# Mask, scale and row maximum of attention scores as one VectorE instruction per tile

## The chip, the cores and the metric

The kernel runs on one core of a Trainium2 chip. The metric is the device time of one execution in microseconds (us); the median of three runs is shown for the kernel before.

## The reference, cut to what matters

The input x has 4 sequences of 512 tokens with 512 features. Each token is normalised (layer norm), and the result goes two ways.

- Causal attention with 16 heads of 128 features: `scores = q @ k.T / sqrt(128)`, masked scores are set to -1e5, `attn = softmax(scores)`, `z = attn @ v`, and the heads are summed through `W_O`.
- A gated feed-forward network of 1408 hidden features with ternary weights, `silu(g) * u`, projected back and passed through silu.

The output is `x + attention * silu(ffn)`. All inputs and the output are f32.

## The kernel before, in words

The feed-forward part comes first (about the first 270 us). Then come 64 attention **units**, one for each pair of sequence and head. Every f32 operand of a matmul is held as two f16 parts, "hi" and "lo", and a product is three f16 matmuls. ScalarE (ACT) writes the hi part, VectorE (DVE) writes the lo part as the difference.

TensorE (PE) runs in `unit(u)`: the projections Q and K of head u+1 (`project_head`), V of a later tile (`project_v(u + 4)`), the scores of head u+1 (`scores`), an output projection (`project_out_tile(u - 4)`) and last `weigh_v(u)`, the product of the softmax of head u with V. So the softmax of a head has about one unit of time before PE needs it. Before `scores`, PE waits for the exponentials of the head before (`exp_ok`) and for Q and K of this head (`q_lo`, `k_lo`). `weigh_v` waits for two DMA transposes of the probabilities, hi (`pt_ok[0]`) and lo (`pt_ok[1]`).

The causal scores of one head lie in three PSUM banks as four tiles, listed in `SCORE_TILES` in the order in which PE writes them: query block 3 (512 wide, first bank), query block 2 (384 wide, second bank), query block 0 (128 wide, the rest of the second bank), query block 1 (256 wide, third bank). `score_mm` counts three steps for them, because block 2 gives no signal of its own.

The softmax of a head passes through these steps, and the queues of the engines hold them in this order:

- DVE `maxima`: add the mask on the diagonal blocks (L1056, three instructions), reduce each tile to its row maximum (L1062, four), multiply the maxima by the negative scale (L1066, two: tile 0 alone, then the other three together).
- ACT `exps`: four exponentials from PSUM with `neg_max` as bias and a row sum (L824). Then ACT `split_probs`: the hi part of the probabilities (L837, four).
- DVE `invert_sums` (L1072, two), then `add_out` (L1094, the output accumulation, which also releases GpSimd), then DVE `split_probs`: the lo part (L1080, four).
- SyncE (SP) issues the two transposes (L335) when all hi parts and then all lo parts are there. It also loads one slice of weights for each unit.
- Behind them on DVE come the lo parts of Q (L1040) and K (L1043) of the next head, of Z (L1087), of V (L1049) and of a weight slice (L898).

Units 60 to 62 have no V projection, and in them the lo part of Z (L1087) comes ahead of the lo parts of Q and K. Unit 60's output projection waits for it.

GpSimd (POOL) fetches x and the parked feed-forward result for finished tiles from about 900 us on, combines them with two elementwise instructions for each tile (L383, L386) and stores them. For the last four tiles it prepares a base with eight instructions in a row (L414, L416). At the start it builds `ident` and `mask`.

Of the kernel before, what the change touches and what calls it, by code (L numbers as in the profile page):

```python
# [28 lines left out]
ALU = mybir.AluOpType  # L29
ACT = mybir.ActivationFunctionType  # L30
AX_X = mybir.AxisListType.X
F32 = mybir.dt.float32
# [3 lines left out]
P = 128  # L36
B, S, D = 4, 512, 512
# [4 lines left out]
TT = S // P  # L42
# [7 lines left out]
WS = 16.0  # L50
SCORE_SCALE = float(E) ** -0.5 / WS ** 2
MASKED = -1.0e5 / SCORE_SCALE
EPS = 1e-5


SCORE_TILES = [(3, 0, 0, 0), (2, 1, 0, 512), (0, 1, 384, 896), (1, 2, 0, 1024)]
P_AT = {i: at for i, _, _, at in SCORE_TILES}

DIAGONALS = [(0, 384, 1), (1, 256, 2), (2, 128, 1)]

# [20 lines left out]
def build(nc, x, ffn_w, attn_w, cols, b_o, down_s, out):  # L83
# [7 lines left out]
    with ExitStack() as ctx:  # L91
        def sb(name, shape, dt):
            return ctx.enter_context(nc.sbuf_tensor(name, shape, dt))

        def sem(name):
            return ctx.enter_context(nc.semaphore(name))
# [10 lines left out]
        fw, at = carve(group, 2 * MT * 3 * 512)  # L107
        FW = [fw.rearrange("p (s m w n) -> p s m w n", s=2, m=MT, w=3)[:, part] for part in (0, 1)]
        x_in, at = carve(at, TT * D, F32)
        ffn_in, at = carve(at, 2 * 3 * 512, F32)  # L110
        silu_gate, at = carve(at, S, F32)
        hidden, at = carve(at, S, F32)
        ht, at = carve(at, 2 * 3 * S)
# [40 lines left out]
        K = [sb(f"K_{n}", [P, S], F16) for n in ("hi", "lo")]  # L154
        w_in = sb("w_in", [P, 2, 512], F32)
        ident = sb("ident", [P, P], F32)
        mask = sb("mask", [P, 2, P], F32)
        cols_in = sb("cols_in", [P, 3 * H + 2 * MT], F32)
        biases = sb("biases", [P, 3 * H], F32)
        ffn_scales = sb("ffn_scales", [P, 2 * MT], F32)  # L160
# [12 lines left out]
        newton_a = sb("newton_a", [P, TT], F32)  # L173
        newton_b = sb("newton_b", [P, TT], F32)
        rstd = sb("rstd", [P, TT], F32)
        row_max = sb("row_max", [P, TT], F32)
        neg_max = sb("neg_max", [P, TT], F32)
        row_sum = sb("row_sum", [P, TT], F32)
        inv_sum = sb("inv_sum", [P, TT], F32)
# [62 lines left out]
        out_mm = sem("out_mm")  # L242
        out_added = sem("out_added")
        score_mm = sem("score_mm")
        masked = sem("masked")
        maxed = sem("maxed")
        negated = sem("negated")
        exp_ok = sem("exp_ok")
        inverted = sem("inverted")
        p_hi = sem("p_hi")  # L250
# [100 lines left out]
        @block.gpsimd  # L351
        def _(pool):
            nc.gpsimd.memset(ident[:], 0.0).then_inc(blank_ok, 1)
            nc.gpsimd.memset(mask[:], 0.0).then_inc(blank_ok, 1)
            nc.gpsimd.memset(ones[:], 1.0).then_inc(ident_ok, 1)
            pool.wait_ge(blank_ok, 2)
            nc.gpsimd.affine_select(out=ident[:], in_=ident[:], compare_op=ALU.not_equal, fill=1.0, base=0,
                                    pattern=[[-1, P]], channel_multiplier=1).then_inc(ident_ok, 1)
            nc.gpsimd.affine_select(out=mask[:], in_=mask[:], compare_op=ALU.is_ge, fill=MASKED, base=0,
                                    pattern=[[0, 2], [-1, P]], channel_multiplier=1).then_inc(ident_ok, 1)  # L360
            pool.wait_ge(const_loaded, 48)
            nc.gpsimd.tensor_scalar(ffn_scales[:], cols_in[:, 3 * H:], 1.0 / WS, None, ALU.mult).then_inc(const_scaled, 1)
            nc.gpsimd.tensor_scalar(biases[:], cols_in[:, 0:3 * H], WS, None, ALU.mult).then_inc(const_scaled, 1)
            nc.gpsimd.tensor_scalar(down_rows[:], down_rows[:], 1.0 / WS, None, ALU.mult).then_inc(const_scaled, 1)

            pool.wait_ge(score_mm, 1)
            for part in (0, 1):
                for at, blocks in GAPS:
                    nc.gpsimd.memset(P_SPLIT[part][:, at:at + blocks, :], 0.0).then_inc(gaps_ok, 1)
            pool.wait_ge(park_done, 16 * B)  # L370
            with pool.Fori(0, T // P) as t:
                nc.gpsimd.tensor_copy(acc[:, t], b_o_rows[:]).then_inc(acc_ready, 1)


            def load_tail(t, par):
                pool.dma_start(x_again[:, par], x_tiles[t]).then_inc(tail_loaded[par], 16)
                pool.dma_start(silu_again[:, par], parked_tiles[t]).then_inc(tail_loaded[par], 16)

            def finish(t, par, turns):

                pool.wait_ge(tail_loaded[par], 32 * turns)
                pool.wait_ge(out_added, TAIL_ADDED + t + 1)
                nc.gpsimd.tensor_tensor(silu_again[:, par], acc[:, t], silu_again[:, par],  # L383
                                        ALU.mult).then_inc(tail_mul, 1)
                pool.wait_ge(tail_mul, t + 1)
                nc.gpsimd.tensor_tensor(silu_again[:, par], silu_again[:, par], x_again[:, par],  # L386
                                        ALU.add).then_inc(tail_add, 1)
                pool.wait_ge(tail_add, t + 1)
                pool.dma_start(out_tiles[t], silu_again[:, par]).then_inc(stored[par], 16)

            def refill(t, par, turns):
                pool.wait_ge(stored[par], 16 * turns)
                load_tail(t, par)

            pool.wait_ge(v_mm, TAIL_ADDED)
            pool.wait_ge(q_mm, TAIL_ADDED)
            for par in range(2):
                load_tail(par, par)
            with pool.Fori(0, TT // 2) as i:
                for par in range(2):  # L400
                    finish(2 * i + par, par, i + 1)
                    refill(2 * i + par + 2, par, i + 1)


            pool.dma_start(x_last, x_chunks[B - 1]).then_inc(last_loaded, 16)
            pool.dma_start(silu_last, parked_chunks[B - 1]).then_inc(last_loaded, 16)
            with pool.Fori(TT // 2, TT) as i:
                for par in range(2):
                    finish(2 * i + par, par, i + 1)
                    refill(2 * i + par + 2, par, i + 1)  # L410

            pool.wait_ge(last_loaded, 32)
            for t in range(TT):
                nc.gpsimd.tensor_tensor(acc[:, TAIL + t], acc[:, TAIL + t], silu_last[:, t], ALU.mult).then_inc(base_mul, 1)  # L414
                pool.wait_ge(base_mul, t + 1)
                nc.gpsimd.tensor_tensor(acc[:, TAIL + t], acc[:, TAIL + t], x_last[:, t], ALU.add).then_inc(base_ok, 1)  # L416
            for par in range(2):
                finish(2 * TT + par, par, TT + 1)
                refill(2 * TT + par + 2, par, TT + 1)
            for par in range(2):  # L420
                finish(TAIL - 2 + par, par, TAIL // 2)
            for t in (0, 1):
                pool.wait_ge(last_mul, t + 1)
                nc.gpsimd.tensor_tensor(silu_last[:, t], silu_last[:, t], acc[:, TAIL + t],
                                        ALU.add).then_inc(pool_sum, 1)
            for par in range(2):
                pool.wait_ge(stored[par], 16 * (TAIL // 2))
# [274 lines left out]
        def _(act):  # L702
# [114 lines left out]
                nc.scalar.activation(V[0][:, (t // TT) % 2, t % TT, :], v_bank(t)[:], ACT.Copy).then_inc(v_hi, 1)  # L817

            def exps(n):
                for i, b_, col, at in SCORE_TILES:  # L820
                    width = (i + 1) * P
                    if i >= TT - 2:
                        act.wait_ge(negated, 2 * n + TT - i)
                    e = nc.scalar.activation(probs[:, at:at + width], SC[b_][:, col:col + width], ACT.Exp,  # L824
                                             bias=neg_max[:, i:i + 1], scale=SCORE_SCALE,
                                             accum_out=row_sum[:, i:i + 1])
                    if i in (TT - 1, 1):
                        e.then_inc(exp_ok, 1)
# [54 lines left out]
        def _(dve):  # L883
# [167 lines left out]

            def maxima(n):

                for b_, col, blocks in DIAGONALS:
                    dve.wait_ge(score_mm, 3 * n + b_ + 1)
                    nc.vector.tensor_tensor(SC[b_][:, col:col + blocks * P], SC[b_][:, col:col + blocks * P],  # L1056
                                            mask[:, 0:blocks, :].rearrange("p b k -> p (b k)"),
                                            ALU.add).then_inc(masked, 1)
                for g, (i, b_, col, _) in enumerate(SCORE_TILES):
                    if g < 3:  # L1060
                        dve.wait_ge(masked, 3 * n + g + 1)
                    nc.vector.reduce_max(row_max[:, i:i + 1], SC[b_][:, col:col + (i + 1) * P], AX_X).then_inc(maxed, 1)  # L1062
                    if g in (1, TT - 1):
                        dve.wait_ge(maxed, TT * n + (1 if g == 1 else TT))
                        cols_ = slice(TT - 1, TT) if g == 1 else slice(0, TT - 1)
                        nc.vector.tensor_scalar(neg_max[:, cols_], row_max[:, cols_], -SCORE_SCALE, None,  # L1066
                                                ALU.mult).then_inc(negated, 1)

            def invert_sums(n):
                for half, cols_ in enumerate((slice(TT - 1, TT), slice(0, TT - 1))):  # L1070
# [118 lines left out]
```

## Time and profile before

| | |
|---|---|
| time, median of 3 runs | 1154.16 us (1153.47 to 1157.09) |
| span of the profiled execution | 1154.1 us, mean granted TensorE clock 0.995 |
| PE matmul busy | 1125.5 us, 98% |
| DVE busy | 729.6 us, 63% |
| ACT busy | 575.7 us, 50% |
| POOL busy | 84.1 us, 7% |
| chain that ended last | PE 88%, DVE 3%, DMA 3%, ACT 3%, issue 2% |

The profile gives no time of its own for that execution beside the span from its first to its last instruction. Busy time is what an engine spent in instructions. The chain that ended last follows the work back from the last instruction, at each step to what released it, so it names what set the end.

### The profile page before, as it was taken

To read this page: it belongs to the slowest core of one execution; us is meant where nothing else is said; L and a number is where in the kernel's file an instruction comes from. 1 tells how busy PE (TensorE), PEld (TensorE's weight loads), DVE (VectorE), ACT (ScalarE), POOL (GpSimd) and SP (SyncE) were. 2 spreads that over 40 slices of the span, in tenths; PEclk is the share of its full clock that TensorE was granted. 3 is DMA by queue.
4 is the path that set the end of the run, shared out by engine and by line. 5 is a ranking of instruction groups with operands and counts; after the bars stand their busy time and mean duration, and the time that the engine had idled before them with its cause. 6 is when DMAs were issued, how large, how long until landed. Compare 5 with 4: busy or idle time off the path is not lost.

```text
span 1154.1 us, 23252 instructions
## 1 busy us (share of the span) xinstructions
PE 1125.5 (98%) x5772; PEld 547.8 (47%) x5772; DVE 729.6 (63%) x1587; ACT 575.7 (50%) x1276; POOL 84.1 (7%) x104
## 2 busy tenths in 40 slices
PE   5999999999999999999999999999999999999987
PEld 3344444444444544544444545444445454554443
DVE  6665364435776666666666666666666666677775
ACT  5754353334565544555455545555555444455532
POOL 1000000003000000000000000000000000134373
PEclk9999999999999999999999999999999999999989
DMA  6401111112444334333444334333444633346545
GB/s 227 167 30 43 45 56 55 55 48 64 97 92 89 82 77 82 82 77 77 85 89 87 77 77 86 77 77 80 88 90 80 114 60 59 86 114 187 118 118 132
DMA packets 236756, 101.77 MB, mean 88 GB/s; under 512 B 219456, under 2 KB 219456, under 8 KB 236736
## 3 DMA queue, kind: packets, MB, share of 16 engines
q1 hardware_dynamic: 231200, 85.78, 33.9%
q0 software_dynamic: 3424, 11.54, 3.3%
q10 hardware_dynamic: 2112, 4.19, 1.0%
q8 instruction: 12, 0.20, 0.1%
q14 instruction: 8, 0.07, 0.0%
HBM read 38.57 MB, written 8.39 MB: 41 GB/s over the span
## 4 chain that ended last, share of the span: by engine, by line
PE 88%; DVE 3%; DMA 3%; ACT 3%; issue 2%; SPq 0%; ACTq 0%; DVEq 0%
PE bank L436 79%; PE bank L589 8%; DMA arena<-arena 2%; PE bank L449 1%; ACT arena L824 1%; ACT arena L837 1%; DMA arena<-ffn_w_dram 1%; DVE row_max L1062 1%; DVE arena L1080 0%; SPq L335 0%; DMA arena<-x_dram 0%; DVE bank L1056 0%; DVE arena L888 0%; ACT V_hi L817 0%; DVE arena L1147 0%
## 5 line engine op out<-in xcount | busy, mean ns | idle before, releaser
L436 PE MATMUL bank<-XT_hi,arena 128*128 (+1 forms) x1392 | 453.3, 380 | 2.8 <-issue 2.7
L436 PE MATMUL bank<-XT_lo,arena 128*128 (+1 forms) x864 | 328.0, 380 | 0.0
L436 PE MATMUL bank<-arena 128*128 (+1 forms) x1124 | 268.3, 380 | 1.2 <-DVE arena L1087 1.0
L824 ACT ACTIVATE arena<-bank,neg_max 128x512 f32<-128x512 f32 (+3 forms) x256 | 132.6, 524 | 216.2 <-DVE neg_max L1066 216.1
L436 PEld LDWEIGHTS bank<-XT_hi,arena 128*128 (+1 forms) x1392 | 136.4, 98 | 161.9 <-issue 7.0
L436 PEld LDWEIGHTS bank<-arena 128*128 (+1 forms) x1124 | 107.6, 98 | 126.2 <-issue 13.4
L436 PE MATMUL bank<-arena,XT_hi 128*128 (+1 forms) x512 | 152.3, 379 | 0.0
L1080 DVE SCALAR_TENSOR_TENSOR arena<-arena,inv_sum 128x512 f16<-128x512 f32 (+3 forms) x256 | 144.2, 625 | 4.3 <-ACT arena L837 4.3
L436 PEld LDWEIGHTS bank<-XT_lo,arena 128*128 (+1 forms) x864 | 84.7, 98 | 92.7 <-issue 0.8
L837 ACT ACTIVATE arena<-arena,inv_sum 128x512 f16<-128x512 f32 (+3 forms) x256 | 122.3, 558 | 0.8 <-DVE inv_sum L1072 0.8
L589 PE MATMUL bank<-arena,V_hi 128*128 128x512 f16 x504 | 111.0, 301 | 3.3 <-DMA arena<-arena 3.0
L1062 DVE TENSOR_REDUCE row_max<-bank 128x1 f32<-128x512 f32 (+3 forms) x256 | 111.1, 481 | 0.0
L436 PE MATMUL bank<-arena,XT_lo 128*128 (+1 forms) x256 | 97.0, 379 | 0.0
L813 ACT ACTIVATE K_hi<-bank,biases 128x512 f16<-128x512 f32 x64 | 44.0, 687 | 100.6 <-PE bank L436 100.5
L1043 DVE SCALAR_TENSOR_TENSOR K_lo<-bank,biases,K_hi 128x512 f16<-128x512 f32 x64 | 48.0, 750 | 72.2 <-ACT K_hi L813 72.2
L817 ACT ACTIVATE V_hi<-bank 128x512 f32 (+1 forms) x64 | 38.2, 597 | 91.4 <-PE bank L436 91.4
L1049 DVE TENSOR_TENSOR V_lo<-bank,V_hi 128x512 f32 (+1 forms) x64 | 44.3, 692 | 58.8 <-ACT V_hi L817 58.8
L957 DVE SCALAR_TENSOR_TENSOR arena<-bank,ffn_scales,arena 128x512 f32<-128x512 f32 x44 | 33.0, 751 | 74.8 <-PE bank L436 65.5
L436 PEld LDWEIGHTS bank<-arena,XT_hi 128*128 (+1 forms) x512 | 50.0, 98 | 60.4 <-DVE V_lo L1049 0.2
L436 PE MATMUL bank<-K_hi,Q_hi 128*128 128x512 f16 (+3 forms) x256 | 74.0, 302 | 3.7 <-DVE K_lo L1043 3.7
L436 PE MATMUL bank<-K_lo,Q_hi 128*128 128x512 f16 (+3 forms) x256 | 77.3, 302 | 0.0
L1072 DVE RECIPROCAL inv_sum<-row_sum 128x1 f32<-128x1 f32 (+1 forms) x128 | 21.6, 170 | 86.9 <-ACT arena L824 80.0
(83 smaller groups left out, 1085.8 us busy)
## 6 DMA issues: line engine op xcount, KB each, us to landing
w_in<-attn_w_dram SPq DMA_DIRECT2D x64, 256.0 KB, 2.6
arena<-ffn_w_dram SPq DMA_DIRECT2D x11, 768.0 KB, 5.3
arena<-x_dram SPq DMA_DIRECT2D x16, 256.0 KB, 4.0
parked_silu<-arena ACTq DMA_DIRECT2D x4, 1024.0 KB, 4.5
arena<-x_dram POOLq DMA_DIRECT2D x12, 256.0 KB, 2.9
arena<-parked_silu POOLq DMA_DIRECT2D x12, 256.0 KB, 3.0
out_dram<-arena POOLq DMA_DIRECT2D x12, 256.0 KB, 2.8
arena<-arena SPq DMA_TRANSPOSE x128, 4.2
```

Of the source, the lines that this page charges most:

```text
L436: mm = nc.tensor.matmul(out, stationary(a, k), moving(b, k), start=first and n == 0 and i == 0, stop=last and n == len(tiles) - 1 and i == ...
L589: return nc.tensor.matmul(ZB[:, j * P:], V[a][:, (u // HG) % 2, j, ds((u % HG) * E, E)], PT[b][:, (J_STEP + 1) * j:J_STEP * j + TT, :].rea ...
L813: nc.scalar.activation(K[0][:], KB[:], ACT.Identity, bias=bias_of(1, n)).then_inc(k_hi, 1)
L817: nc.scalar.activation(V[0][:, (t // TT) % 2, t % TT, :], v_bank(t)[:], ACT.Copy).then_inc(v_hi, 1)
L824: e = nc.scalar.activation(probs[:, at:at + width], SC[b_][:, col:col + width], ACT.Exp, bias=neg_max[:, i:i + 1], scale=SCORE_SCALE, accu ...
L837: nc.scalar.activation(query_blocks(0, i), probs_by_block(i, at), ACT.Copy, scale=inv_sum[:, i:i + 1]).then_inc(p_hi, 1)
L957: nc.vector.scalar_tensor_tensor(out=hidden, in0=UP[:], scalar=ffn_scales[:, ds(MT + m, 1)], in1=silu_gate, op0=ALU.mult, op1=ALU.mult).th ...
L1043: nc.vector.scalar_tensor_tensor(out=K[1][:], in0=KB[:], scalar=bias_of(1, n), in1=K[0][:], op0=ALU.add, op1=ALU.subtract).then_inc(k_lo, 1)
L1049: nc.vector.tensor_tensor(V[1][:, at, t % TT, :], v_bank(t)[:], V[0][:, at, t % TT, :], ALU.subtract).then_inc(v_lo, 1)
L1062: nc.vector.reduce_max(row_max[:, i:i + 1], SC[b_][:, col:col + (i + 1) * P], AX_X).then_inc(maxed, 1)
L1072: nc.vector.reciprocal(inv_sum[:, cols_], row_sum[:, cols_]).then_inc(inverted, 1)
L1080: nc.vector.scalar_tensor_tensor(out=query_blocks(1, i), in0=probs_by_block(i, at), scalar=inv_sum[:, i:i + 1], in1=query_blocks(0, i), op ...
```

## The change

`maxima` has one instruction for each of the four tiles in place of three mask additions, four reductions and two small multiplications. The new instruction adds the mask to the whole tile, multiplies by the negative scale, writes the result in place in PSUM and keeps the minimum of each row, starting at `NO_MIN`. The exponential then uses a scale of -1. The mask grows from two diagonal blocks to a row of 512 columns whose last 128 are the diagonal block and the rest zero, so a tile of any width takes its last columns. Ahead of three of the four instructions DVE waits for the scores and counts up a semaphore `minimizing` that nobody waits for. The exponential of tile 1 now waits for tile 2 as well, since both lie in one bank.

```diff
+NO_MIN = 3.0e38
-DIAGONALS = [(0, 384, 1), (1, 256, 2), (2, 128, 1)]
+MAX_AFTER = [1, 2, 2, 3]
+EXP_AFTER = [1, 3, 3, 4]
...
-        mask = sb("mask", [P, 2, P], F32)
+        mask = sb("mask", [P, S], F32)
...
-            nc.gpsimd.affine_select(out=mask[:], in_=mask[:], compare_op=ALU.is_ge, fill=MASKED, base=0,
-                                    pattern=[[0, 2], [-1, P]], channel_multiplier=1).then_inc(ident_ok, 1)
+            nc.gpsimd.affine_select(out=mask[:, S - P:], in_=mask[:, S - P:], compare_op=ALU.is_ge, fill=MASKED, base=0,
+                                    pattern=[[-1, P]], channel_multiplier=1).then_inc(ident_ok, 1)
...
             def exps(n):
-                for i, b_, col, at in SCORE_TILES:
+                for g, (i, b_, col, at) in enumerate(SCORE_TILES):
                     width = (i + 1) * P
-                    if i >= TT - 2:
-                        act.wait_ge(negated, 2 * n + TT - i)
+                    if g != 2:
+                        act.wait_ge(maxed, TT * n + EXP_AFTER[g])
                     e = nc.scalar.activation(probs[:, at:at + width], SC[b_][:, col:col + width], ACT.Exp,
-                                             bias=neg_max[:, i:i + 1], scale=SCORE_SCALE,
+                                             bias=neg_max[:, i:i + 1], scale=-1.0,
                                              accum_out=row_sum[:, i:i + 1])
...
             def maxima(n):
 
-                for b_, col, blocks in DIAGONALS:
-                    dve.wait_ge(score_mm, 3 * n + b_ + 1)
-                    nc.vector.tensor_tensor(SC[b_][:, col:col + blocks * P], SC[b_][:, col:col + blocks * P],
-                                            mask[:, 0:blocks, :].rearrange("p b k -> p (b k)"),
-                                            ALU.add).then_inc(masked, 1)
                 for g, (i, b_, col, _) in enumerate(SCORE_TILES):
-                    if g < 3:
-                        dve.wait_ge(masked, 3 * n + g + 1)
-                    nc.vector.reduce_max(row_max[:, i:i + 1], SC[b_][:, col:col + (i + 1) * P], AX_X).then_inc(maxed, 1)
-                    if g in (1, TT - 1):
-                        dve.wait_ge(maxed, TT * n + (1 if g == 1 else TT))
-                        cols_ = slice(TT - 1, TT) if g == 1 else slice(0, TT - 1)
-                        nc.vector.tensor_scalar(neg_max[:, cols_], row_max[:, cols_], -SCORE_SCALE, None,
-                                                ALU.mult).then_inc(negated, 1)
+                    width = (i + 1) * P
+                    if g != 2:
+                        dve.wait_ge(score_mm, 3 * n + MAX_AFTER[g])
+
+                        dve.sem_inc(minimizing, 1)
+                    nc.vector.tensor_tensor_reduce(
+                        out=SC[b_][:, col:col + width], in0=SC[b_][:, col:col + width], in1=mask[:, S - width:],
+                        scale=-SCORE_SCALE, scalar=NO_MIN, op0=ALU.add, op1=ALU.min,
+                        accum_out=neg_max[:, i:i + 1]).then_inc(maxed, 1)
```

## Rows read from the trace of the kernel before

**Rows 1.** The page's first part: busy time, share of the span, instructions.
```profile
PE 1125.5 (98%) x5772; PEld 547.8 (47%) x5772; DVE 729.6 (63%) x1587; ACT 575.7 (50%) x1276; POOL 84.1 (7%) x104
```

**Rows 2.** The chain that ended last: start us, us, what.
```profile
340.07 11.99 PE bank L436 x60
...
869.62 1.63 PE bank L589 x12
```

**Rows 3.** Waits of PE over the span: us in total, times, longest us.
```profile
PE bank L449 <- DVE arena L920: 9.8, 1, 9.8
PE bank L436 <- DVE K_lo L1043: 3.7, 3, 3.4
PE bank L589 <- DMA arena<-arena: 3.0, 3, 1.6
```

**Rows 4.** Timeline of DVE in a steady unit: start us, us, instruction.
```profile
704.89 0.82 DVE L1056 TENSOR_TENSOR bank<-bank,mask 128x128 f32<-128x128 f32 x3
...
707.39 0.17 DVE L1066 TENSOR_SCALAR neg_max<-row_max 128x3 f32<-128x3 f32 x1
...
714.00 0.75 DVE L1043 SCALAR_TENSOR_TENSOR K_lo<-bank,biases,K_hi 128x512 f16<-128x512 f32 x1 [1.35 <-ACT K_hi L813]
```

**Rows 5.** Timeline of ACT and of PE in the same unit.
```profile
706.86 0.69 ACT L824 ACTIVATE arena<-bank,neg_max 128x512 f32<-128x512 f32 x1 [3.32 <-DVE neg_max L1066]
707.59 0.58 ACT L824 ACTIVATE arena<-bank,neg_max 128x384 f32<-128x384 f32 x1
...
708.95 1.91 ACT L837 ACTIVATE arena<-arena,inv_sum 128x512 f16<-128x512 f32 x4
```
```profile
715.42 0.38 PE L436 MATMUL bank<-K_hi,Q_hi 128*128 128x512 f16 x1
```

**Rows 6.** Groups of instructions, shapes apart: count | busy us, mean ns.
```profile
L1094 DVE SCALAR_TENSOR_TENSOR arena<-bank,arena 128x512 f32 x59 | 40.8, 692 | 9.8 <-PE bank L436 3.0
L1056 DVE TENSOR_TENSOR bank<-bank,mask 128x128 f32<-128x128 f32 x128 | 37.3, 291 | 1.2 <-PE bank L436 1.2
```
```profile
L824 ACT ACTIVATION_READ_ACCUMULATOR arena<-bank,neg_max 128x1 f32 x256 | 50.6, 198 | 0.0
```

**Rows 7.** The chain at three transposes, in different units.
```profile
309.66 4.28 DMA arena<-arena
```
```profile
903.23 10.43 DMA arena<-arena
```
```profile
1126.32 6.78 DMA arena<-arena
```

**Rows 8.** Timeline of PE at its two waits near the end.
```profile
1098.52 2.76 PE L436 MATMUL bank<-arena 128*128 128x512 f16 x12 [0.95 <-DVE arena L1087]
...
1115.67 0.58 PE L436 MATMUL bank<-K_hi,Q_hi 128*128 128x512 f16 x1 [3.36 <-DVE K_lo L1043]
```

**Rows 9.** Timeline of DVE in the unit between them.
```profile
1102.11 0.29 DVE L1056 TENSOR_TENSOR bank<-bank,mask 128x128 f32<-128x128 f32 x1
...
1104.93 1.22 DVE L1066 TENSOR_SCALAR neg_max<-row_max 128x3 f32<-128x3 f32 x1
...
1108.39 5.15 DVE L1080 SCALAR_TENSOR_TENSOR arena<-arena,inv_sum 128x512 f16<-128x512 f32 x4 [0.52 <-ACT arena L837]
```

**Rows 10.** Timeline of ACT and of POOL there (POOL: one of eight).
```profile
1106.19 0.58 ACT L824 ACTIVATE arena<-bank,neg_max 128x384 f32<-128x384 f32 x1 [1.01 <-DVE neg_max L1066]
```
```profile
1104.87 1.27 POOL L414 TENSOR_TENSOR arena<-arena 128x512 f32<-128x512 f32 x1
```

**Rows 11.** Windows: us, busy (x) of PE, PEld, DVE, ACT, POOL, clock, DMA share, GB/s.
```profile
911.85:913.70 1.85, 0.22 (x5) 0.05 (x2) 0.35 (x4) 1.85 (x8) 0.00 (x0) 1.00 1.11 290
```
```profile
1112.30:1114.00 1.70, 0.01 (x1) 0.00 (x0) 1.70 (x2) 0.00 (x0) 1.70 (x2) 1.00 0.31 58
1114.00:1115.60 1.60, 0.00 (x0) 0.00 (x0) 1.60 (x4) 0.00 (x0) 1.52 (x2) 0.65 0.51 101
```
```profile
1115.70:1121.70 6.00, 6.00 (x25) 3.08 (x26) 3.54 (x11) 1.11 (x3) 3.56 (x6) 0.53 0.58 162
```

More of the change, by code:

```diff
@@ L175, in build @@
         rstd = sb("rstd", [P, TT], F32)
-        row_max = sb("row_max", [P, TT], F32)
         neg_max = sb("neg_max", [P, TT], F32)
@@ L244, in build @@
         score_mm = sem("score_mm")
-        masked = sem("masked")
+        minimizing = sem("minimizing")
         maxed = sem("maxed")
-        negated = sem("negated")
         exp_ok = sem("exp_ok")
```

## The prediction

> **What bounds the kernel now.** The page comes first: PE is busy for 98% of the span and DVE for 63% [rows 1], so DVE is not the bound as a whole. The chain that ended last says where in time that holds. A steady unit is two pieces that touch, 1.63 us of softmax times V and 11.99 us of everything else, 13.62 us in all, and this pair repeats without a gap: from the first row to the last (869.62-340.07-11.99)/13.62 = 38.0 units lie between them [rows 2]; the chain shows some 12 more such units behind 929 us. In these units nothing that DVE or ACT does earlier can shorten the kernel. So I read next the list of what PE waited for. Behind the one for the first x, two kinds have the softmax ahead of them: 3.7 us for the lo part of K and 3.0 us for transposes of probabilities [rows 3]; a third, for the lo part of Z, comes up in the timeline. The chain places the three transposes: one in the first loop units, one at 903 us, where the landing took 10.43 us instead of 4.28, one at 1126 with 6.78 [rows 7]. The timeline of PE has the two other waits near the end, 0.95 us for Z and 3.36 for K [rows 8]. The windows show one cost more: in the longer of these gaps the granted clock fell, and the next 6.0 us ran at 0.53, which is about the 1.2 GHz level instead of 2.4 [rows 11]. The change can win only in these places; anywhere else it can only lose.
>
> **What the change removes and adds in a unit.** I measure from T0, the start of the first mask addition, 704.89. Before, the first exponential starts at T0+1.97, the second at T0+2.70, and the hi parts of the probabilities at T0+4.06 [rows 4, 5]. From the second exponential to the hi parts it is 1.36 us of ACT work that stays. Nine DVE instructions go.
>
> Four come. No row shows the new instruction. The nearest one by its operands is the mask addition itself, PSUM and SBUF in, PSUM out, 291 ns for 128 columns; the addition of an output tile, which also has two f32 inputs, takes 692 ns for 512 [rows 6]. The slope is (692-291)/384 = 1.04 ns per column, so I take 692, 558, 424 and 291 ns for widths 512, 384, 256 and 128. In a row of three such additions 291+291+424 = 1006 ns took 0.82 us [rows 4], so each starts about 0.09 us before the one ahead is over. The row minimum has to be read out; ACT has a row of its own for that, 198 ns [rows 6]. I take 0.10 us on DVE for it, with 0 below and 0.20 above. The two semaphore instructions ahead of three of them go through the queue while the instruction before still runs; I cost them at nothing, and the upper 0.20 covers them where it doesn't hide them.
>
> Then the first tile is done at T0+0.69+0.10 = 0.79. The second starts at 0.70 and ends at 1.36, the third (128 wide) ends at 0.70+0.57+0.29+0.10 = 1.66, the fourth at 2.09. The second exponential waits for the third tile, so it starts at T0+1.70 instead of 2.70, and the hi parts follow at T0+3.06; the fourth exponential would start at 2.61, after the fourth tile. **The softmax gains g = 1.0 us**, with 1.24 if the read-out costs nothing (the exponentials themselves then set the pace) and 0.7 if it costs 0.20. If an instruction ran at half the rate per column, the third tile would end near 2.72 and g would be about -0.1.
>
> The wider mask costs POOL one longer fill and a narrower selection near the start; PE's first transposes wait 9.8 us for x [rows 3], and that covers it. What the exponential reads and its scale value don't change its length.
>
> **Where g counts.** In the steady units not at all. There DVE still has 1.35 us of idle time ahead of the lo part of K [rows 4].
>
> At the first loop units PE waits for the transpose that landed at 309.66+4.28 = 313.94, about 0.6 us (of 3.0 us in three waits the one behind the 903 us transpose is the longest, 1.6; the timeline splits the other 1.4 into 0.6 here and 0.7 at 1133), and 0.2 us for K, by what is left of 3.7 in its other two waits [rows 3, 7]. SP issues the transposes right after the hi and lo parts, so they move by g: gain 0.7.
>
> At 903 us the lo transpose shared the DMA engines with four loads that POOL issues when PE has done a projection. That moment doesn't move, the transpose does, so g is a lower bound if it gets ahead of some of the loads and PE's wait of 1.6 us [rows 3], 2.4 with the gaps beside it, is the upper one: gain 1.0, ends 0 and 2.4.
>
> Unit 60: its lo part of Z comes behind the lo parts of the probabilities. These move by g, POOL's work beside them too, since it is released by the output addition ahead of them. The wait of 0.95 us goes: gain 0.95.
>
> Unit 61, in times of before (all of it is 0.95 earlier): T0 is 1102.11. Here the small multiplication by the negative scale took 1.22 us instead of 0.17 [rows 4, 9]; it ended just when POOL's instruction ended, 1104.87+1.27 = 1106.14 [rows 10], while mask additions and reductions ran at their usual length beside POOL. So the second exponential started at 1106.19 [rows 10]. Without that instruction it starts at T0+1.70 = 1103.81, **2.4 us earlier**. The trace shows that a DVE instruction with both tensors in SBUF takes turns with POOL: the four lo parts took 5.15 us instead of 1.93, one turn of POOL each [rows 9]. Started at 1106.0 instead of 1108.39 they meet the same turns, end of turn 1106.14 and then one about each 1.3 to 1.6 us, and end near 1111.3 instead of 1113.5. Gain 2.2, and PE's wait of 3.36 becomes 1.15, with K done at 1113.3.
>
> The skill says the same of those turns: by the Trainium skill, GPSIMD Engine Reference, Key points, GpSimd shares its SBUF interfaces with VectorE and the two contend when a DVE instruction runs in a 2-port mode or has two SBUF inputs. By that rule the new instruction (one input in PSUM) doesn't take turns, as the mask addition doesn't here; if it did, its three later instructions would each wait for a turn, and the gain of 2.2 would shrink to nearly nothing.
>
> The clock: in that gap it was still 1.00 from 1112.30 to 1114.00, with PE idle, and 0.65 on average until 1115.60; in the gap of 1.63 us at 912 it stayed at 1.00 [rows 11]. If PE starts again at 1113.45, before the fall, the half-speed stretch goes too. It held softmax times V, 1.63 us at full clock [rows 2], and the scores, which are as many columns, so 3.26 us of work in 6.0 us [rows 11]: gain 2.75.
>
> Unit 62 starts 4.95 us earlier within its frame. Its last transposes need to land before PE has done two projections and an output, as before, when PE waited 0.7 us for a landing of 6.78 us [rows 7]. The chain to them has gained more than PE there (g on top), but POOL's loads meet them: gain 0.3, ends 0.7 and -1.5.
>
> Sum: 0.7 + 1.0 + 0.95 + 2.2 + 2.75 + 0.3 = 7.9 us. The span of the profiled execution is 1154.1, 0.1 below the median of the runs shown, so 1154.1 - 7.9 = **1146.2 us**.
>
> **Rivals.**
>
> *The clock falls all the same, or a late transpose takes its place.* For it: the margin between 1113.45 and the fall near 1114.5 is about 1 us, and the landing of the last transposes varies from 4.3 to 10.4 us [rows 7]. Against it: nothing shows that shorter gaps make the clock fall. It costs 2.75 again: 1149. Still faster than before by 0.4%.
>
> *Half rate.* With g at -0.1 nothing is won up to unit 60. In unit 61 the second exponential starts at T0+2.76, still 1.3 us earlier because the 1.22 us turn is gone; the lo parts are done 0.7 to 1.2 us earlier and the clock's fall is a toss-up: 1150.5 to 1153.5, say 1152. The rows of two f32 inputs at full rate [rows 6] speak against it, but none of them keeps a running minimum. The Trainium skill speaks for it in one place and against in another. The Vector Engine (DVE) Microarchitecture Reference, Points that are easy to get wrong, says that a two-source instruction with two non-bf16 SBUF sources runs at half throughput, since no port is left for the accumulator; here one source is in PSUM. DVE: opcode table, instruction layouts, handler registers and perf-mode slots, Datapath and trigger behaviour, says that a stage that reads its own previous result has no bubble. By the first the time would be 1152, by the second 1146; no run so far shows which.
>
> *A high fixed cost per instruction makes it slower.* Let each new instruction cost d more than I take. The hi parts start at the later of T0+3.06+3d and T0+2.58+4d. DVE can be later by 1.35 us (its idle time ahead of K) plus about 0.5 (K is done at 714.00+0.75, PE's scores start at 715.42 [rows 4, 5]) before PE waits in every unit. So it decides from d = 0.83 us on: four instructions of 1.2 to 1.6 us. At d = 1.0 it is (6.58-4.06-1.85) = 0.67 us for each of some 58 units, 39 us: 1193. No DVE row that isn't behind POOL has such a fixed cost; the row of 128 columns has 0.16 us beside the columns [rows 6].
>
> *It gives nothing.* The gaps are filled by something else that ends as late (Q and K wait for ACT, the transposes for DMA): 1153 to 1154. Against it: in unit 61 DVE, not ACT or a DMA, is what works without a pause through PE's gap, 1.70 of 1.70 and 1.60 of 1.60 us [rows 11].
>
> **Chances.** My forecast 0.55, own range 1144.2 to 1148; clock or transpose 0.17; half rate 0.13; no gain 0.08; slower 0.07. The rest of the doubt is in the size of g. Faster by over 0.3% (below 1150.7; that is about what a measurement of this kernel can tell from no change) takes the first two and a little of the half rate less some of the second: 0.71. Same 0.22, slower 0.07. The range from 1144.0 to 1153.0 reaches to the half rate and leaves out the slower cases and half of those without gain.
>
> **What would show each step.** The new DVE rows should read near 690, 560, 290 and 420 ns with a read-out of about 0.1 each; from the first to the hi parts 3.1 us in a steady unit instead of 4.06. Steady units stay at 13.62 us. PE's wait for Z at 1098 should be gone, that for K about 1.1 us, and the granted clock at 1.00 through the next stretch. Rows near 1220 ns for 512 columns would be the half rate; rows that end with POOL's would be turns. I am wrong above all if the clock falls in the shorter gap or if transposes near 903 or 1133 land later than now.

## The result, and the profile after

The changed kernel takes 1146.05 us (median of 4 runs, 1144.51 to 1147.55). The kernel before, with a fourth run, takes 1155.59 us (1153.47 to 1157.09). The ratio is 0.9918, 95% interval 0.9900 to 0.9935, so it is faster by 0.8%. The forecast was 1146.2 us. The profiled execution of the changed kernel took 1144.51 us, the fastest of its four; its span is 1143.2 us, 10.9 us less than the profiled span of before.

The page's first part, to be held against [rows 1]:

```profile
PE 1121.1 (98%) x5772; PEld 546.9 (48%) x5772; DVE 674.4 (59%) x1523; ACT 581.4 (51%) x1276; POOL 84.6 (7%) x104
```

DVE has lost 55 us of busy time and the kernel 9.5 us in the medians. The rest became idle time of DVE beside a busy PE: the chain still consists of pairs of 11.99 and 1.63 us. From the start of the first row here to the start of the last unit shown, (868.23-337.05)/13.62 = 39.0 units pass, so none of them is longer than 13.62 us, as in [rows 2]. What ended last (start us, us, what):

```profile
337.05 11.99 PE bank L436 x60
...
868.23 11.99 PE bank L436 x60
...
899.03 11.37 DMA arena<-arena
...
1107.63 0.67 DVE K_lo L1043
```

The last two rows are the two places that are still late: a transpose of probabilities near 900 us, and K in unit 61. PE's waits over the span (total us, times, longest) show the same, beside [rows 3]:

```profile
PE bank L449 <- DVE arena L920: 9.5, 1, 9.5
PE bank L544 <- ACT lo_abs L714: 2.1, 1, 2.1
PE bank L436 <- issue: 1.9, 4, 0.6
PE bank L589 <- DMA arena<-arena: 1.9, 1, 1.9
PE bank L436 <- DVE K_lo L1043: 0.8, 1, 0.8
```

The waits for K went from 3.7 us in three to 0.8 in one, those for transposes from 3.0 in three to 1.9 in one, and the wait for Z [rows 8] is gone.

The new instruction by shape (count | busy us, mean ns | idle before it), which stands where [rows 6] had the mask addition:

```profile
L1060 DVE CUSTOM_DVE_ANT_0 bank<-bank,mask 128x512 f32<-128x512 f32 x64 | 44.3, 691 | 0.5 <-PE bank L436 0.5
...
L1060 DVE CUSTOM_DVE_ANT_0 bank<-bank,mask 128x384 f32<-128x384 f32 x64 | 38.1, 596 | 0.0
L1060 DVE DVE_READ_ACCUMULATOR2_ANT neg_max<- 128x1 f32 x256 | 35.8, 140 | 0.0
...
L1060 DVE CUSTOM_DVE_ANT_0 bank<-bank,mask 128x256 f32<-128x256 f32 x64 | 29.6, 462 | 0.0
```

512 columns take 691 ns; 692 was expected and 1220 would have been half rate. Each instruction has a second row, the read-out of its minimum. The timeline of DVE in a steady unit shows how they lie (start us, us):

```profile
701.86 0.69 DVE L1060 CUSTOM_DVE_ANT_0 bank<-bank,mask 128x512 f32<-128x512 f32 x1
702.47 0.14 DVE L1060 DVE_READ_ACCUMULATOR2_ANT neg_max<- 128x1 f32 x1
702.47 0.60 DVE L1060 CUSTOM_DVE_ANT_0 bank<-bank,mask 128x384 f32<-128x384 f32 x1
702.98 0.14 DVE L1060 DVE_READ_ACCUMULATOR2_ANT neg_max<- 128x1 f32 x1
702.98 0.33 DVE L1060 CUSTOM_DVE_ANT_0 bank<-bank,mask 128x128 f32<-128x128 f32 x1
703.23 0.14 DVE L1060 DVE_READ_ACCUMULATOR2_ANT neg_max<- 128x1 f32 x1
703.23 0.46 DVE L1060 CUSTOM_DVE_ANT_0 bank<-bank,mask 128x256 f32<-128x256 f32 x1
```

and that of ACT beside it:

```profile
702.64 0.69 ACT L824 ACTIVATE arena<-bank,neg_max 128x512 f32<-128x512 f32 x1 [2.13 <-DVE neg_max L1060]
...
703.40 0.58 ACT L824 ACTIVATE arena<-bank,neg_max 128x384 f32<-128x384 f32 x1
...
704.77 1.91 ACT L837 ACTIVATE arena<-arena,inv_sum 128x512 f16<-128x512 f32 x4
```

A read-out starts together with the next instruction, 0.61 us after its own began, so in the row of four it takes no time of its own. The first exponential starts 0.17 us behind the read-out's start. From the first instruction to the hi parts it is 704.77-701.86 = 2.91 us, where it was 4.06 and 3.06 was forecast: the softmax gained **1.15 us, not 1.0**.

Unit 61, the expensive one [rows 8 to 10], in DVE's timeline:

```profile
1097.48 0.70 DVE L1060 CUSTOM_DVE_ANT_0 bank<-bank,mask 128x512 f32<-128x512 f32 x1
...
1098.61 0.33 DVE L1060 CUSTOM_DVE_ANT_0 bank<-bank,mask 128x128 f32<-128x128 f32 x1
...
1101.16 5.16 DVE L1076 SCALAR_TENSOR_TENSOR arena<-arena,inv_sum 128x512 f16<-128x512 f32 x4 [0.43 <-ACT arena L837]
```

in POOL's and in PE's:

```profile
1098.99 1.26 POOL L416 TENSOR_TENSOR arena<-arena 128x512 f32<-128x512 f32 x1
```
```profile
1108.44 0.38 PE L436 MATMUL bank<-K_hi,Q_hi 128*128 128x512 f16 x1 [0.77 <-DVE K_lo L1043]
```

The new instructions run beside POOL at their usual length, and the lo parts (5.16 us) still take turns with it. The windows over the gap and what follows (columns as in [rows 11]) show the granted clock at 1.00, that is the 2.4 GHz level, through both:

```profile
1107.65:1108.44 0.79, 0.02 (x1) 0.03 (x1) 0.79 (x2) 0.00 (x0) 0.79 (x1) 1.00 1.09 214
1108.44:1112.00 3.56, 3.56 (x26) 2.27 (x27) 2.38 (x10) 1.77 (x7) 3.18 (x4) 1.00 0.38 70
```

**Where the 10.9 us of span went.** I take as the start of a unit the first 512-wide matmul of softmax times V in PE's timeline, and compare the lengths of the units in both traces.

| stretch | before, us | after, us | difference |
|---|---|---|---|
| start of unit 0 (feed-forward part and first projections) | 289.64 | 288.27 | 1.4 |
| first loop units 1 to 4 | 11.14, 11.33, 12.21, 13.96 | 11.03, 11.03, 11.30, 13.62 | 1.7 |
| steady units | 13.62 each | 13.62 each | 0 |
| units 46 to 48 (transpose near 900 us) | 14.11, 16.07, 13.89 | 13.62, 16.34, 13.62 | 0.5 |
| units 60, 61, 62 | 12.15, 16.07, 12.36 | 11.03, 11.97, 11.03 | 1.1 + 4.1 + 1.3 |
| rest, after the start of unit 62 | | | 0.8 |

Of the first row's 1.4 us, 1.04 were there at the end of the feed-forward part, which the change doesn't touch. The same start lies between 287.7 and 289.9 us in the experiments' traces, so I put that part down to variation of single executions. The medians differ by 9.5 us and not by 10.9, mainly because the profiled execution of the changed kernel was 1.5 us faster than its median.

The last row is one wait. In the timelines of PE, before and after, the lo half of unit 62's product with V starts:

```profile
1133.15 0.72 PE L589 MATMUL bank<-arena,V_hi 128*128 128x512 f16 x4 [0.71 <-DMA arena<-arena]
```
```profile
1122.18 0.71 PE L589 MATMUL bank<-arena,V_hi 128*128 128x512 f16 x4
```

That is 1133.15-1131.18 = 1.97 us behind the start of the unit's product before and 1122.18-1121.10 = 1.08 after it: the wait for the last transpose is gone.

### The profile page after: what moved, and what is told of

Same layout as the page of the kernel before. It is cut to its first block, busy times and chain, and to the rows that moved or that the text cites. A ratio compares the mean times of both kernels' runs of the same rounds, so it can differ in the third digit from the quotient of the medians.

```text
span 1143.2 us, 23441 instructions
## 1 busy us (share of the span) xinstructions
PE 1121.1 (98%) x5772; PEld 546.9 (48%) x5772; DVE 674.4 (59%) x1523; ACT 581.4 (51%) x1276; POOL 84.6 (7%) x104
## 4 chain that ended last, share of the span: by engine, by line
PE 94%; DMA 2%; DVE 1%; ACT 1%; issue 1%; SPq 0%; DVEq 0%; ACTq 0%
PE bank L436 85%; PE bank L589 9%; DMA arena<-arena 1%; PE bank L449 1%; DMA arena<-ffn_w_dram 1%; DMA arena<-x_dram 0%; DVE arena L888 0%; ACT arena L837 0%; ACT arena L824 0%; DVE arena L1143 0%; SPq L335 0%; ACT lo_abs L714 0%; DVE arena L1076 0%; DVE stats L906 0%; DVE arena L1147 0%
## 5 line engine op out<-in xcount | busy, mean ns | idle before, releaser
L1060 DVE CUSTOM_DVE_ANT_0 bank<-bank,mask 128x512 f32<-128x512 f32 (+3 forms) x256 | 117.5, 520 | 0.5 <-PE bank L436 0.5
L1040 DVE SCALAR_TENSOR_TENSOR Q_lo<-bank,biases,Q_hi 128x512 f16<-128x512 f32 x64 | 47.9, 748 | 60.3 <-ACT Q_hi L811 60.1
L811 ACT ACTIVATE Q_hi<-bank,biases 128x512 f16<-128x512 f32 x64 | 43.9, 686 | 73.4 <-PE bank L436 73.4
```

Source lines behind the costliest of these rows:

```text
L811: nc.scalar.activation(Q[0][:], QB[:], ACT.Identity, bias=bias_of(0, n)).then_inc(q_hi, 1)
L1040: nc.vector.scalar_tensor_tensor(out=Q[1][:], in0=QB[:], scalar=bias_of(0, n), in1=Q[0][:], op0=ALU.add, op1=ALU.subtract).then_inc(q_lo, 1)
L1060: nc.vector.tensor_tensor_reduce(out=SC[b_][:, col:col + width], in0=SC[b_][:, col:col + width], in1=mask[:, S - width:], scale=-SCORE_SCA ...
```

## Experiments

All ratios are against the kernel before, run beside the experiment on the same chip. That kernel's own median was 1155.59 us beside the changed kernel and 1154.55, 1154.63 and 1156.75 us in three later series (single runs from 1153.20 to 1157.82), so a difference between times of two series is uncertain by 1 us or more. No kernel leaves out work of the reference.

### The new instruction only in the last three units, or everywhere but there

The first kernel uses the new instruction for heads 61 to 63 only, the second for heads 0 to 60 only. The other heads have the old nine instructions. The edit is the same, with two constants swapped:

```diff
-                maxima(u + 1)
+                maxima(u + 1, FUSE if v else FUSE_TAIL, 0 if v else N0)
...
-                exps(u + 1)
+                exps(u + 1, FUSE if v else FUSE_TAIL, 0 if v else N0)
```

> The new instruction only for the last three heads (61 to 63), all others as before. If the gain comes from single places and most of it from unit 61 (no small multiplication that waits for POOL's turn, a shorter gap on PE, no fall of the clock), PE's gap for K is about 1 us instead of 3.36, the clock stays at 1.00 through it, and the kernel is 5.5 to 7 us faster than before (ratio about 0.9945). If every unit contributed its shorter softmax, three heads of 64 would give at most 0.5 us (ratio 0.9995).

> The new instruction for heads 0 to 60, the last three as before. By my theory 2.0 us come back in the first loop units, 0.5 at the late transpose, 1.1 in unit 60, together 3.6 us (ratio about 0.997); PE's gap for K stays above 3 us and the clock falls in it. If the gain were spread over all units this kernel would have nearly all of it, 9 us (ratio 0.992).

Measured: the last heads alone give 1148.86 us, ratio 0.9953 (0.9940 to 0.9967), 5.7 us less than before. All heads but these give 1153.01 us, 0.9984 (0.9975 to 0.9993), 1.5 us less for 61 of 64 heads. In the second kernel the gap for K is back at its old 3.36 us, in PE's timeline:

```profile
1112.71 0.39 PE L446 MATMUL bank<-K_hi,Q_hi 128*128 128x512 f16 x1 [3.36 <-DVE K_lo L1055]
```

and the window behind it has the fallen clock:

```profile
1112.70:1118.70 6.00, 5.99 (x29) 3.20 (x30) 3.69 (x11) 1.07 (x3) 3.57 (x6) 0.72 0.59 155
```

So most of the gain lies in three heads. The traces say where the rest is: the first loop units 1 to 4 take 48.49 us in the first kernel and 46.97 in the second, where the whole change took them from 48.64 to 46.98. The first kernel's unit 61 is 11.96 us (before 16.07) and its unit 60 the old 12.15, because the wait for Z there stands behind head 60, which has the old instructions; the second kernel's unit 60 is 11.03. The second kernel's gain is well below the 3.6 us that were expected. The two gains add to 7.2 us where the whole change has 9.5. The late transpose is part of that: its unit, 16.07 us before and 16.34 after the change, is 17.74 in the first kernel and 16.99 in the second. Another 1.0 us is the kernel before, which took 1154.55 us here and 1155.59 beside the changed kernel.

### A small multiplication put back in the last units

After the four new instructions of heads 61 to 63 stands one multiplication of the minima by 1.0, for which the exponentials of tiles 1 to 3 wait, as they did before for the scale.

```diff
+                if tail:
+                    dve.wait_ge(maxed, TT * n + TT)
+                    nc.vector.tensor_scalar(neg_copy[:, 0:TT - 1], neg_max[:, 0:TT - 1], 1.0, None,
+                                            ALU.mult).then_inc(negated, 1)
```

> The changed kernel, with one small SBUF to SBUF multiplication of three columns put back behind the fourth tile in the last three heads; the exponentials of tiles 1 to 3 wait for it. If such an instruction waits for POOL's turn, it takes about 0.9 us instead of 0.17 in unit 61, the lo parts of the probabilities take a later turn, and PE's gap for K grows from 0.8 to 2.0 us: 1.2 us slower than the changed kernel, and about 4 us slower if that gap already lets the clock fall. If the turn didn't matter and only the number of instructions did, it costs 0.3 us.

Measured: 1148.98 us, 0.9950 (0.9936 to 0.9963), 2.9 us more than the changed kernel took in its own series. DVE's timeline in unit 61, then POOL's, then PE's:

```profile
1102.38 0.88 DVE L1070 TENSOR_SCALAR neg_copy<-neg_max 128x3 f32<-128x3 f32 x1
```
```profile
1101.97 1.27 POOL L418 TENSOR_TENSOR arena<-arena 128x512 f32<-128x512 f32 x1
```
```profile
1112.70 0.38 PE L438 MATMUL bank<-K_hi,Q_hi 128*128 128x512 f16 x1 [2.08 <-DVE K_lo L1047]
```

Three columns take 0.88 us, to 1103.26, and POOL's instruction ends at 1103.24. The gap for K grows from 0.77 to 2.08 us, and units 61 and 62 by 1.30 and 0.70 us (PE waits for K once more there, 0.5 us). So the old multiplication's turn behind POOL was a cost of its own, 2.0 us over the two units. The rest of the 2.9 us isn't from it: the unit of the late transpose took 18.85 us in this trace, 2.5 more than after the change. The windows over the gap and behind it say something about the clock:

```profile
1110.55:1112.70 2.15, 0.07 (x1) 0.03 (x1) 2.15 (x5) 0.00 (x0) 2.15 (x2) 1.00 0.42 82
1112.70:1116.00 3.30, 3.30 (x25) 2.13 (x26) 2.64 (x11) 0.93 (x3) 2.06 (x3) 1.00 0.50 113
```

With PE idle for 2.08 us the clock stayed at 1.00; with 3.36 us, before and in the second kernel above, it fell. The margin that the forecast counted on is there.

By the Trainium skill, GPSIMD Engine Reference, Key points, GpSimd contends with DVE instructions that have two SBUF inputs or run in a 2-port mode. The traces agree as far as they go: the new instruction, with one input in PSUM, kept its 0.70 and 0.33 us beside POOL, and the lo parts, with two inputs in SBUF, did not keep their 1.93. The multiplication has one tensor as input, in SBUF, and did not keep its 0.17 either; in which mode it ran no run shows.

### POOL's loads moved away from the transpose near 900 us

POOL issues four loads at 898.7 to 901.1 us; the transpose issued at 899.03 took 11.37 us. One more wait lets the loads start after the scores of a later head:

```diff
             pool.wait_ge(q_mm, TAIL_ADDED)
+            pool.wait_ge(score_mm, 3 * (TAIL_ADDED + 1))
```

> The changed kernel, but POOL issues its first four loads (1 MB) only when PE has written the scores of the next head, instead of after a Q projection. If these loads are what makes the lo transpose land in 11.4 us instead of 4.3, PE's unit of 16.34 us at 911 us becomes 13.62 and the kernel is 2.7 us faster than the changed one. If the transpose is late for another reason, or the loads then meet the next transposes, it is the same within 1 us.

Measured: 1142.62 us, 0.9898 (0.9883 to 0.9914). PE no longer waits for a transpose anywhere, and all units there are 13.62 us. I ran it again beside the changed kernel on one chip:

> The changed kernel as it is, on the same chip as the versions beside it. It should be 9 to 10 us faster than before, with the unit at 911 to 923 us between 15 and 19 us long.

> The changed kernel with POOL's first loads behind the scores, again, beside the changed kernel on one chip: 2.5 to 5 us faster than it, because only the late transpose at 903 us is taken away and that one costs 2.7 to 5.2 us from run to run.

1146.00 us (1143.19 to 1146.76) and 1142.88 us (1142.38 to 1143.41), so the late transpose costs 3.1 us after the change, and more than half of the spread between runs goes with it (from 3.6 to 1.0 us).

### How much room DVE has in a steady unit

In units 4 to 47 a reduction whose result nobody reads stands ahead of the first new instruction, over 2304 or 3328 columns.

```diff
+                    if g == 0 and wide:
+                        dve.wait_ge(idled, n - 4)
+                        nc.vector.reduce_max(idle_max[:], XT[0].rearrange("p k t -> p (k t)")[:, 0:wide],
+                                             AX_X).then_inc(idled, 1)
```

> The changed kernel with one more DVE reduction of 2304 columns (about 2.5 us, by 1.04 ns per column) ahead of the first new instruction in the 44 units of the loop from 4 to 48; its result is not used. By my theory the softmax may come 1.85 us later than before and 3.0 us later than now before PE waits, so these units stay at 13.62 us; only the transpose beside POOL's loads may land later, 0 to 3 us in all. If DVE's chain did bound the steady units, the kernel would be 100 us slower.

> The same with 3328 columns (about 3.5 us). That is 0.5 us beyond the 3.0 us of slack: the 44 units should read 14.1 to 14.2 us instead of 13.62 and the kernel be 20 to 27 us slower than the changed one. If the slack is larger than I read from the rows, nothing changes; if it is used up much earlier, the kernel is slower by more than 40 us.

Measured: 1146.57 us, 0.9927 (0.9903 to 0.9950), and 1150.52 us, 0.9961 (0.9946 to 0.9976). With the shorter one, DVE's timeline and the window over the 41 steady units behind unit 4:

```profile
702.42 2.54 DVE L1064 TENSOR_REDUCE idle_max<-XT_hi 128x1 f32<-128x2304 f16 x1
```
```profile
349.43:907.90 558.47, 558.47 (x2953) 278.43 (x2951) 436.27 (x862) 292.87 (x697) 2.37 (x4) 1.00 0.41 83
```

PE is busy in 558.47 of 558.47 us: 2.54 us more on DVE in each of 44 units cost nothing. With the longer one (3.61 us) PE waits for K in its steady units, from the list of its waits:

```profile
PE bank L438 <- DVE K_lo L1045: 5.5, 23, 0.8
```

The 44 units take 608.29 us instead of 44 x 13.62 = 599.3, 0.20 us each, far from the 0.5 us and the 20 to 27 us in all that were expected. Their lengths alternate between 13.62 and 13.99 us; why only every second one waits isn't shown. The softmax starts 3.53 us later in them (707.69 to 711.22), so the room is about 3.53-0.20 = 3.3 us; from the rows of before, 1.35+0.5 and the gain of 1.15 make 3.0. The kernel's median is only 4.0 us above that of the shorter one, not 9.0, at least in part because the two units at the late transpose take 28.28 us in this trace and 32.89 in the other.

### The kernel before, with POOL's instructions spread out

Before, POOL's eight instructions for the last tiles stand in a row just where unit 61 runs. Here each pair follows one of the finished tiles, with the old softmax:

```diff
                     refill(2 * i + par + 2, par, i + 1)
+                    t = 2 * i + par - TT
...
+                    nc.gpsimd.tensor_tensor(acc[:, TAIL + t], acc[:, TAIL + t], silu_last[:, t], ALU.mult).then_inc(base_mul, 1)
+                    pool.wait_ge(base_mul, t + 1)
+                    nc.gpsimd.tensor_tensor(acc[:, TAIL + t], acc[:, TAIL + t], x_last[:, t], ALU.add).then_inc(base_ok, 1)
```

> The kernel before, unchanged on DVE, ACT and PE; POOL prepares the base of the last four tiles one tile at a time behind the four finishes of its second loop, instead of eight instructions in a row beside unit 61. If POOL's turns are what made the long gap, the small multiplication takes 0.17 us again, the lo parts 1.9 us in unit 61, PE's gap for K of 3.36 us and the clock's fall go, and the kernel is 5 to 6 us faster than before with none of the new instructions. If the nine DVE instructions themselves make that gap, at most 1 us is gained.

> The changed kernel with POOL's first loads behind the scores and the base prepared early as well. PE should have no wait for K or Z left in the last units: the unit of 12.0 us becomes 11.03, 1 us faster than with the later loads alone (ratio to before about 0.989), and the fastest of all versions.

Measured, without the change: 1150.78 us, 0.9962 (0.9948 to 0.9976). DVE's timeline in unit 61, where the corresponding rows of before are 1.22 and 5.15 us [rows 9]:

```profile
1105.90 0.27 DVE L1067 TENSOR_SCALAR neg_max<-row_max 128x3 f32<-128x3 f32 x1
...
1108.41 1.94 DVE L1081 SCALAR_TENSOR_TENSOR arena<-arena,inv_sum 128x512 f16<-128x512 f32 x4 [0.52 <-ACT arena L838]
```

The gap for K and the fall of the clock are gone, though no instruction of the softmax was changed; unit 61 takes 12.13 us instead of 16.07. The gain of 3.9 us is below the 5 to 6 expected: PE waits for two transposes near the end instead, 0.93 and 1.20 us, and the unit of the late one is 17.65 us long. The second kernel has the change, the later loads and this order. It takes 1146.18 us, 0.9917 (0.9903 to 0.9931), no better than the change alone and not the fastest, as was expected. Its K and Z are never late, but a transpose is, as the chain, POOL's timeline and PE's timeline show:

```profile
1101.75 9.25 DMA arena<-arena
```
```profile
1102.71 0.54 POOL L376 DMA_DIRECT2D arena<-x_dram  x1 [2.47 <-DMA out_dram<-arena]
1103.24 0.54 POOL L377 DMA_DIRECT2D arena<-parked_silu  x1
```
```profile
1111.05 0.55 PE L591 MATMUL bank<-arena,V_hi 128*128 128x512 f16 x2 [3.25 <-DMA arena<-arena]
```

POOL, free earlier, now issues two loads 1.0 and 1.5 us behind the transpose, and it lands after 9.25 us.

### All three POOL edits, with and without the change

A third edit holds the two refills back that met that transpose:

```diff
                 finish(2 * TT + par, par, TT + 1)
+                pool.wait_ge(z_mm, 62)
                 refill(2 * TT + par + 2, par, TT + 1)
```

> The changed kernel with POOL's first loads behind the scores, the base prepared early, and the loads for the last two tiles held back until PE has used the transposes of head 61. In the kernel with only the first two edits these last loads made one transpose land after 9.3 us and PE wait 3.3 us. If the loads are the cause, the unit of 16.3 us becomes 11.03 and the kernel is the fastest of all, 1141.5 to 1142.5 us. If the transposes near the end are late for another reason, it stays near 1146.

> The kernel before with the same three edits on POOL and none of the new instructions. What is left between this kernel and the one above is what the new instruction gives with POOL out of its way: by my sums 2.0 us in the first loop units and 1 to 2 us in units 60 to 62, so this one is at 1145 to 1147 us. If the instruction's gain doesn't need POOL, the two differ by 8 us or more.

Measured: with the change 1141.06 us (1140.50 to 1141.25), 0.9867 (0.9851 to 0.9882), the fastest kernel of this study. Without it 1145.12 us (1144.88 to 1145.35), 0.9902 (0.9887 to 0.9918). PE's waits with the change have no K, no Z and no transpose of probabilities left:

```profile
PE bank L452 <- DVE arena L923: 9.2, 1, 9.2
PE bank L547 <- ACT lo_abs L717: 2.3, 1, 2.3
PE bank L439 <- issue: 2.0, 3, 1.2
```

Three edits of POOL's order gain as much as the change does, on the same chip (1145.12 against 1146.00). Where they have taken the collisions away, the new instruction is still worth 1145.12-1141.06 = 4.1 us: unit 60 (12.16 to 11.03), unit 62 (11.56 to 11.03), and about 1.6 us in the first loop units, 3.3 us in all; another 0.5 us lies ahead of unit 0's start, where single executions differ by more than that.

## Why the prediction was right, by its steps

**The mechanism** was right: nothing in steady units, and the gain at the softmax chain's few late places. The sum of 7.9 us compares with 9.5 us between the medians. That the time came out within 0.2 us is luck: the forecast took 7.9 us from 1154.1, and the median of before with its fourth run is 1155.59. A base 1.5 us too low made up for a gain 1.6 us too small. The 1154.1 was a span, and in every profiled execution that has both, the time is 1.3 us above the span; that it lay so close to the median of the three first runs was a coincidence.

| term | forecast, us | measured, us |
|---|---|---|
| first loop units | 0.7 | 2.0 |
| transpose near 903 us | 1.0 (0 to 2.4) | 0.5 |
| unit 60, Z | 0.95 | 1.1 |
| unit 61, gap for K | 2.2 | 3.36-0.77 = 2.6 |
| the clock | 2.75 | 4.1+1.3-2.6 = 2.8 |
| unit 62 and the end | 0.3 | 0.8 |
| sum | 7.9 | 9.8 |

The measured column comes from two single executions, which is why its sum isn't the 9.5 us of the medians.

- **The new instruction's price** was right: 691 ns for 512 columns. These rows refute the rivals of half rate and of a high fixed cost. The rule that the forecast set for half rate asks for two inputs in SBUF; here one is in PSUM, so this case doesn't test it, and the forecast should not have counted it for that rival. The room that the second rival needed to use up was a little larger than I took: about 3.3 us from the new state, where the forecast's 1.85 from before makes 3.0.
- **The read-out** was mis-sized. I put 0.10 us behind each instruction; the row is 140 ns, but it overlaps the next instruction. That is the 1.15 instead of 1.0.
- **First loop units, mis-sized term.** I added up the waits in the rows, 0.6 and 0.2 us. Over units 1 to 4 the windows have PE idle for 1.12 us before and 0.10 after, and busy for 47.52 us before and 46.88 after, with 254 matmul records in each. Together 1.66 us, and 0.33 ahead of unit 1. The listed waits missed the small gaps. The 0.64 us of busy time are probably short stalls that the matmul rows, whose ends are modelled, cover; that isn't shown. The length of a unit from start to start shows both.
- **The late transpose, mis-sized term.** The transpose was issued 1.17 us earlier relative to PE (5.36 us behind the start of unit 45's product with V, before 6.53), but it landed in 11.37 us instead of 10.43, so 0.2 us remained there; the other 0.3 is a short gap in the unit behind it, which is gone. That POOL's loads make it late was right: with them moved, the wait is gone and 3.1 us with it. The forecast's upper end (2.4) was below what was to be had, and the change couldn't reach it, since the transpose stayed among the loads.
- **Unit 61** was right in both parts, with one statement too broad: that a DVE instruction with both tensors in SBUF takes turns with POOL. The old multiplication of one column at 1104.22 took 0.14 us in the middle of a POOL instruction (1103.64 to 1104.91), and the reciprocal of three at 1107.70 took 0.17 during another; only the multiplication of three columns and the lo parts waited. In times of before (after's plus 4.63 us, by the start of the unit's softmax) the lo parts end at 1110.95 (forecast 1111.3) and PE starts the scores at 1113.07 (forecast 1113.45). The turn that the small multiplication took behind POOL was a cause of its own: put back, it brought 1.3 us of gap back. So was POOL's row of eight: moved, the old softmax has no such gap.
- **The clock** was right: no fall at a gap of 0.77, none at 2.08, a fall at 3.36 us. The gain is as large as the gap's own, and without it the time would have been about 1149 us (an estimate, 1146.05+2.8).
- **Unit 62 and the end, mis-sized term.** The forecast took 0.3 us of PE's wait of 0.7 for the last transpose; the whole wait is gone, and 0.8 us with it.

**Still open:** why the late transpose varies from run to run (its unit takes 15.59 to 18.85 us in traces with the new instruction and the loads where they were), and with it a part of why the two halves of the change add to only 7.2 us.

## What to carry to other kernels

Ask where PE waits behind the shortened chain, not how much the engine saves: here 55 us of DVE time were worth 9.5, and three heads of 64 held more than half of it. Take the length of each loop turn from start to start in both traces; sums of listed waits can miss half of a loss that is spread in small pieces. Before a forecast is called good to 0.2 us, compare its base and its gain apart: here two errors of about 1.5 us cancelled. Where a chain is late, look at what runs beside it: moving another engine's elementwise work and loads by three edits gained as much as a new instruction, and the two together more, but with only a part of the moves the loads met the next transpose.

## What the runs showed of the hardware that was not expected

- The read-out of a DVE instruction's minimum (140 ns) starts together with the next instruction and delays neither; the first reader, on ACT, started 0.17 us after the read-out began.
- An instruction of 128 rows and three columns, SBUF to SBUF, took 0.88 us (put back in the changed kernel) and 1.22 us (before) beside POOL, up to the end of POOL's instruction; the one of one column (0.14 us) and the reciprocals (0.15 to 0.18 us) in the same stretch kept their length.
- The landing of one DMA transpose went from 4.28 us [rows 7] to 9.25 us with two loads of POOL issued 1.0 and 1.5 us behind it, and to 11.37 us with four, each in one execution.
- One execution's feed-forward part differs from another's by up to 2.2 us (unit 0 starts at 287.7 to 289.9 us), a fifth of the whole effect measured here.
